# Offsets made between the steps of the value projection, half of the columns normalised on GpSimd, far sums turned later

## The chip, the cores and the metric

The kernel runs on one NeuronCore of one Trainium2 chip. A NeuronCore has TensorE (matmuls into PSUM), VectorE, ScalarE and GpSimd (elementwise work) and SyncE, which here only issues DMAs; each works through its own queue in order, and they wait for one another on semaphores. The metric is the time of one execution on the device in microseconds (us), as the median of several runs. Lower is better.

## The reference

The input x is float32, 2 images of 128 channels by 128 by 128 pixels. Two blocks follow each other, each with a residual:

```python
x = x + window_attention(group_norm(x))        # windows of 16 x 16, 8 heads, a bias table
x = x + deformable_conv(group_norm(x))         # the part that the change touches
```

The deformable convolution, with G = 8 groups of 16 channels and K = 9 points (3 x 3):

```python
v  = xt @ value_proj_w.T + value_proj_b                   # value projection
om = xt @ offset_mask_w.T + offset_mask_b                 # per pixel, group, point: dx, dy, mask
loc_x = px + kx + off[..., 0];  loc_y = py + ky + off[..., 1]
# bilinear sample of v at (loc_y, loc_x), four corners, zero outside the image
out = einsum('nhwkgc,nhwkg->nhwgc', sampled, mask)        # sum over the 9 points
out = out @ output_proj_w.T + output_proj_b
```

## The kernel before

The attention block runs first (functions above line 726) and takes about half of the time. `deformable` (line 726) then treats the two images one after the other (`Fori(0, B)` on every engine). For an image:

1. **Projection of the attention's output and the residual.** The sum stays in SBUF as `x1`; `cols` is a view of it by image columns. Group norm statistics are taken on the way; `gn` holds scale and shift of each channel.
2. **Value projection**, 32 steps v of four image columns (`COLS = 4`, `GROUPS = 32`). ScalarE normalises four columns into one half of `d_xn` (line 1357), TensorE multiplies them by the value weights (L1248) into one half of `sum_ps`, VectorE adds the bias into a row buffer in the memory of `vring` (L1460), and SyncE stores it to `vals` in DRAM (L976). There are two row buffers.
3. **A prefix** for the first six groups (`LEAD = 6`). Per group of four columns: TensorE makes offsets and masks (`offsets`, L1257 and L1260) in `om_ps`; ScalarE copies them to `off` (L1381) and takes absolute values (L1384); VectorE looks for far points, those over one pixel off (`find_far`, L1471 to L1476). For groups 0 and 1 ScalarE also makes the hat functions (`hats`, L1390 and L1394), and for group 0 VectorE makes the tap terms (`tap_terms`, L1515 and L1520) and TensorE the tap weights (`weights`, L1270 and L1275). Meanwhile SyncE loads the first seven columns of `vals` into the ring of eight, `vring` (L985), and stores the offsets (L995).
4. **The sampling loop** over 32 groups, written out for eight and looped over in the middle (`each_group`). For each of the four columns r of a group, VectorE multiplies 5 x 5 shifted values by the weights (`products`, L1536, in pieces, into two alternating halves of `prod`), and TensorE adds them up and transposes them into `sum_ps` (`taps`, 25 matmuls, L1297). Between the columns of a group stand, in this order: on TensorE the turn of the far sums of the group before (`turn`, L1307) after column 0, the weights of the next group after 1, the output projection of the group before (`project`, L1315) and the offsets of group q + 7 after 2, with the count of far points (L1285) once per epoch; on VectorE the result of group q - 2 (`result`, L1547) after 0, the tap terms of the next group after 1, the search for far points of group q + 6 after 2, in one group of four also the flags (L1487 to L1496), and after column 3 `read_counts` (L1502), which waits for that count.
5. **Far points.** Once per epoch of four groups GpSimd reads the number of rounds and does them (`far_round`, L1113 to L1163): it fetches one far point per partition and round from DRAM, gathers its corners from `vals`, and scatters the weighted sum into `far_sums`. `far_done` tells that an epoch is finished. SyncE loads a group's far sums into `fsum` (`load_far`, L1006), and waits for `far_done` before it (L1002). All columns that it loads later stand behind this wait in its queue. The groups 0 to 3 are epoch 0; the count of epoch 1 is read in group 1, that of epoch 7 in group 25.
6. **The end**: the last results, then the stores of `x1` to `out`.

GpSimd has nothing to do in steps 2 and 3. The order on each engine is written out by hand.

## Time and profile before

| | |
|---|---|
| Median of 3 runs | 3354.45 us (3354.16 to 3354.75) |
| Profiled execution: time, span | 3350.4 us, 3348.7 us |
| TensorE (PE) busy | 2717.4 us, 81% |
| VectorE (DVE) busy | 2716.9 us, 81% |
| ScalarE (ACT) busy | 1882.3 us, 56% |
| GpSimd (POOL) busy | 1102.7 us, 33% |
| Mean granted TensorE clock | 0.963 of full speed |
| Value projection, image 0 and image 1 begin | 1647.9 us, about 2549.5 us |
| First product of the sampling loop, image 0 and 1 | 1737.5 us, 2640.9 us |
| VectorE waits for "DMA vring<-vals" in the loop | 49.2 us in total |

Busy time says only that an engine executes; what a change is worth is read from the stage, from what ends last there. In the timelines the last part in brackets is the idle time of the engine before the row, and the instruction or transfer that ended it. Several instructions of one line that follow closely are merged, and "x4" tells how many they are.

### The profile page before, as it was taken

The numbers are of one execution on the slowest core, as the hardware profiler recorded it, in microseconds if no ns is written. First come the engines' busy times: TensorE is split into PE (matmuls) and PEld (weight loads), VectorE is DVE, ScalarE is ACT, GpSimd is POOL, SyncE is SP. The second block draws the span as 40 slices with busy tenths as digits, with TensorE's granted clock in tenths as the row PEclk, the third lists the DMA queues.
The fourth block names the chain that finished last, engine by engine and source line by source line (L and its number), as shares of the span: only waits on it lengthen the run. The fifth ranks groups of instructions, "written<-read, shape, count | busy, mean of one in ns | idle before, by whom it ended". The sixth has DMA issues, their size and how long they took to land.

```text
span 3348.7 us, 78453 instructions
## 1 busy us (share of the span) xinstructions
PE 2717.4 (81%) x22424; PEld 2178.8 (65%) x22424; DVE 2716.9 (81%) x6553; ACT 1882.3 (56%) x3529; POOL 1102.7 (33%) x1525
## 2 busy tenths in 40 slices
PE   0599999999999999995665999897856699989886
PEld 0355655565556655563555888887845598888885
DVE  5488888888888888885656999998945599999996
ACT  0488888888888888885262444442204544434420
POOL 0333333333333333332415322135421241115550
PEclk9999999999999999998898999998978899999998
DMA  6788888888888888885642333233365333333334
GB/s 221 126 142 140 146 136 142 139 144 137 143 139 147 136 142 138 141 143 109 199 138 84 99 97 98 93 99 88 89 242 160 110 118 94 96 96 98 105 91 161
DMA packets 350617, 432.47 MB, mean 129 GB/s; under 512 B 42224, under 2 KB 275072, under 8 KB 344304
## 3 DMA queue, kind: packets, MB, share of 16 engines
q1 hardware_dynamic: 338544, 423.85, 56.5%
q0 software_dynamic: 11904, 6.44, 1.6%
q8 instruction: 97, 1.59, 0.2%
q14 instruction: 72, 0.59, 0.1%
HBM read 283.33 MB, written 147.09 MB: 129 GB/s over the span
## 4 chain that ended last, share of the span: by engine, by line
DVE 19%; DMA 8%; issue 8%; PE 6%; POOL 6%; POOLq 2%; DVEq 1%; ACT 1%; SPq 1%; ACTq 0%
DVE prod L1536 11%; DVE tt L1520 2%; PE sum_ps L1297 2%; DMA vring<-vals 2%; DMA vals<-vring 2%; DMA vring<-attended 2%; DVE x L1547 2%; POOL gath L1113 2%; POOLq L1120 1%; PE wt_ps L1275 1%; DMA o_sel<-off_out,pos 1%; DVE my L1515 1%; PE sum_ps L1237 1%; POOL i_sel L1113 1%; PE om_ps L1260 1%
## 5 line engine op out<-in xcount | busy, mean ns | idle before, releaser
L587 ACT ACTIVATE prob<-sbias,nmax 128x256 f32<-128x256 f32 x2048 | 905.0, 501 | 196.1 <-DVE nmax L674 194.1
L1536 DVE TENSOR_TENSOR prod<-vring,wt_ps 128x1920 f32<-128x1920 f32 (+3 forms) x512 | 902.7, 1816 | 58.9 <-DMA vring<-vals 49.2
L674 DVE CUSTOM_DVE_ANT_0 sbias<-s_ps,nbias 128x256 f32<-128x256 f32 x2048 | 766.9, 421 | 224.3 <-PE s_ps L479 211.8
L1297 PE MATMUL sum_ps<-d_ident,prod 128*128 128x128 f32 x6400 | 758.7, 276 | 23.5 <-DVE prod L1536 23.5
L492 PE MATMUL pt_ps<-a_ident,prob 128*128 128x128 f32 x4096 | 644.3, 280 | 134.1 <-ACT prob L587 131.6
L1297 PEld LDWEIGHTS sum_ps<-d_ident,prod 128*128 128x128 f32 x6400 | 721.4, 143 | 38.4 <-DVE prod L1536 31.6
L492 PEld LDWEIGHTS pt_ps<-a_ident,prob 128*128 128x128 f32 x4096 | 447.3, 140 | 277.6 <-DVE probT L683 118.4
L479 PE MATMUL s_ps<-stack 96*128 96x256 bf16 x2048 | 396.2, 274 | 9.5 <-DMA stack<-parts_dram 9.5
L683 DVE COPY probT<-pt_ps 128x512 f32<-128x512 f32 x512 | 351.7, 687 | 11.8 <-PE pt_ps L492 11.7
L423 POOL CAST parts<-qk 128x1024 bf16<-128x1024 f32 x64 | 66.3, 1036 | 860.1 <-ACT qk L580 860.1
L1403 ACT COPY ssum<-sum_ps 128x512 f32<-128x512 f32 x64 | 37.5, 586 | 513.6 <-PE sum_ps L1307 513.6
L1275 PE MATMUL wt_ps<-tt,d_ident 128*128 128x144 f32 x2304 | 312.0, 291 | 0.0
L1275 PEld LDWEIGHTS wt_ps<-tt,d_ident 128*128 128x128 f32 x2304 | 306.9, 195 | 0.9
L479 PEld LDWEIGHTS s_ps<-stack 96*128 96x128 bf16 x2048 | 174.8, 98 | 203.5 <-issue 137.0
L594 ACT COPY probT<-pt_ps 128x512 f32<-128x512 f32 x512 | 290.2, 567 | 0.0
L507 PE MATMUL o_ps<-probT,va 128*32 128x256 f32 x4096 | 274.1, 385 | 0.9 <-DVE probT L683 0.9
L1128 POOL COPY first_e<-first_at 128x2 f32 x16 | 2.8, 178 | 784.3 <-issue 784.3
L1390 ACT ACTIVATE hat<-off,one_col 128x576 f32<-128x576 f32 x128 | 140.5, 1098 | 198.2 <-DVE tt L1520 198.2
L1520 DVE TENSOR_TENSOR tt<-hat,my 128x864 f32<-128x864 f32 x192 | 192.4, 1057 | 9.1 <-PE wt_ps L1275 0.5
L674 DVE DVE_READ_ACCUMULATOR2_ANT nmax<- 128x1 f32 x2048 | 170.8, 83 | 0.0
L1381 ACT COPY off<-om_ps 128x864 f32<-128x864 f32 x64 | 56.3, 880 | 202.6 <-PE om_ps L1260 184.9
L507 PEld LDWEIGHTS o_ps<-probT,va 128*32 128x32 f32 x4096 | 106.9, 109 | 87.8 <-issue 33.9
(166 smaller groups left out, 3489.9 us busy)
## 6 DMA issues: line engine op xcount, KB each, us to landing
stack<-parts_dram SPq DMA_DIRECT2D x768, 128.0 KB, 7.4
vring<-vals SPq DMA_DIRECT2D x270, 320.0 KB
parts_dram<-parts SPq DMA_DIRECT2D x64, 768.0 KB, 6.5
off_out<-off SPq DMA_DIRECT2D x64, 432.0 KB
strips<-x SPq DMA_DIRECT2D x68, 256.0 KB, 3.6
a_stats_in<-x SPq DMA_DIRECT2D x16, 1024.0 KB, 4.9
far_sums<-nothing SPq DMA_DIRECT2D x64, 256.0 KB, 2.1
attended<-on SPq DMA_DIRECT2D x256, 64.0 KB
```

The source lines that it names most:

```text
L479: mm = nc.tensor.matmul(s_ps[:, n % 2, half, :], stack[:, par, 0, h, at:at + P], stack[:, par, 1, h, w * NT:(w + 1) * NT], start=True, sto ...
L492: mm = nc.tensor.transpose(pt_ps[:, T_BANK[n % 4], kh, half * P:(half + 1) * P], prob[:, n % 4, half, kh * P:(kh + 1) * P], ident[:])
L507: mm = nc.tensor.matmul(o_ps[32 * j:32 * j + VA, t * NT:(t + 1) * NT], va[:, par, 2 * w + kh, 4 * t + j, :], probT[:, (4 * k + j) % 8, kh, ...
L587: ins = nc.scalar.activation(prob[:, n % 4, half, :], sbias[:, n % SBIAS, half, :], ACT.Exp, bias=nmax[:, n % SBIAS, half:half + 1], scale ...
L594: nc.scalar.copy(probT[:, n % 8], pt_ps[:, T_BANK[n % 4]]).then_inc(t_read_a, 1)
L674: ins = nc.vector.tensor_tensor_reduce(out=sbias[:, n % SBIAS, half, :], in0=s_ps[:, n % 2, half, :], in1=nbias[:, h, half, :], scale=1.0, ...
L683: nc.vector.tensor_copy(probT[:, n % 8], pt_ps[:, T_BANK[n % 4]]).then_inc(t_read_v, 1)
L1275: mm = nc.tensor.matmul(acc[:, :, jx:jx + KS, jy * G:(jy + KS) * G], ident[:], tt[:, jx, jy, 2 * half:2 * half + 2].rearrange("p r (a k) - ...
L1297: mm = nc.tensor.matmul(sum_ps[:, par, r * H:(r + 1) * H], prod[:, r % 2, dx, dy * C:(dy + 1) * C], ident[:], start=(r + dx + dy == 0), st ...
L1390: nc.scalar.activation(xy(hat[:, j]), xy_off(s), ACT.Abs, bias=0.0 if j == 1 else one_col[:, j // 2:j // 2 + 1]).then_inc(dist_ready, 1)
L1520: ins = nc.vector.tensor_tensor(tt[:, jx], hat[:, jx, :, 0:KG].unsqueeze(1) .to_broadcast([P, 3, COLS, KG]), my[:], ALU.mult)
L1536: nc.vector.tensor_tensor(prod[:, r % 2, first:last].rearrange("p a (t c) -> p (a t) c", c=CG), vring[:, at:at + wide].rearrange("p a (t c ...
```

## The change

- The value projection has four row buffers (`VROWS = 4`) in place of two. Its 32 steps are no longer a loop over pairs but go through `each_step`: eight written out, sixteen in a loop of four, eight written out (`V_FIRST, V_LAST = 8, 24`).
- Odd steps are normalised by GpSimd, even ones by ScalarE, each with a semaphore of its own.
- TensorE makes the offsets of groups 0 to 6 after the value matmuls of steps 1 to 7, from the half of `d_xn` that the step before has used; they are not normalised again. ScalarE reads offsets 0 to 5 in steps 2 to 7; VectorE looks for far points of groups 0 to 4 in steps 3 to 7 and of group 5 in step 24; hats, tap terms, counts and the weights of group 0 are cut up over steps 24 to 31. The prefix is gone.
- SyncE stores offsets in steps 4 to 7 and 24, 25, and loads the first four columns in step 24. GpSimd waits for all stores of values before its far rounds, as SyncE does before the other columns.
- In the loop, the load of the far sums of group q goes from column 2 of group q to column 1 of group q + 1; `turn` of the group before goes from after column 0 to after column 2; `project` is of group q - 2 in place of q - 1, after column 0; `result` goes from after column 0 to after column 2. ScalarE's order in a group is offsets, hats, sums, normalisation; it was offsets, normalisation, sums, hats.

```diff
+VROWS = 4
+V_FIRST, V_LAST = 8, 24
+AHEAD_OFF = LEAD + 1
...
+vrow = vring[:, ATTS:ATTS + VROWS, 0:COLS * C].rearrange("p s (r c) -> p s r c", c=C)
 off = sb("off", [P, RING_O, COLS, KG, 3])
...
+def each_step(eng, body):
+for v in range(V_FIRST):
+    body(v, v % VROWS, v // VROWS)
+with eng.Fori(0, (V_LAST - V_FIRST) // VROWS) as i:
+    for u in range(VROWS):
+        body(VROWS * i + V_FIRST + u, u, i + V_FIRST // VROWS)
+for v in range(V_LAST, GROUPS):
+    body(v, v % VROWS, v // VROWS)
...
-    for n in range(AHEAD_V):
+    def store_values(v, slot, turn):
+        sp.wait_ge(vrow_ready, count(b * GROUPS + v + 2))
+        sp.dma_start(at(vals, ((PAD + v * COLS) * YP + PAD) * C,
+                        [[C, P], [YP * C, COLS], [1, C]]), vrow[:, slot]).then_inc(vrow_out[slot], 16)
+        if isinstance(v, int) and 0 <= v - EPOCH < V_FIRST - EPOCH:
+            store_offsets(first_spot(v - EPOCH))
+        if isinstance(v, int) and 0 <= v - V_LAST < LEAD - (V_FIRST - EPOCH):
+            store_offsets(first_spot(v - V_LAST + V_FIRST - EPOCH))
+        if isinstance(v, int) and v == V_LAST:
+            for n in range(2):
+                sp.wait_ge(vrow_out[n], count(b * (4 * GROUPS) + 16))
+                sp.sem_inc(sp_passed, 1)
+            for n in range(ATTS):
+                load_column(n, n, b * LOADS[n % 2] + n // 2)
+    each_step(sp, store_values)
+    for slot in range(VROWS):
+        sp.wait_ge(vrow_out[slot], count((b + 1) * (4 * GROUPS)))
+        sp.sem_inc(sp_passed, 1)
+    for n in range(ATTS, AHEAD_V):
...
-    for q in range(LEAD):
-        store_offsets(first_spot(q))
...
-            if r == 2:
-                load_far(s)
+            if r == 1 and s.has(-1):
+                load_far(s.on(-1))
     each_group(sp, columns)
+    load_far(first_spot(GROUPS - 1))
     sp.wait_ge(res_ready, count((b + 1) * GROUPS))
...
                 nc.gpsimd.tensor_tensor(rows, rows, bproj_sb[:].unsqueeze(1).to_broadcast([P, COLS, W]),
                                         ALU.add).then_inc(b_added, 1)
+    pool.wait_ge(g_sq, count(2 * b + 2))
+    pool.sem_inc(pool_passed, 1)
+    def normalise(v):
+        pool.wait_ge(v_done, count(b * GROUPS + v))
+        pool.sem_inc(pool_passed, 1)
+        if 2 <= v < AHEAD_OFF + 2:
+            pool.wait_ge(om_done, count(b * GROUPS + v - 1))
+            pool.sem_inc(pool_passed, 1)
+        nc.gpsimd.tensor_scalar(xn[:, 1], cols[:, v * COLS:(v + 1) * COLS, :], gn[:, 0:1], gn[:, 1:2],
+                                ALU.mult, ALU.add).then_inc(vn_ready[1], 1)
+    for v in range(1, GROUPS, 2):
+        normalise(v)
+    for slot in range(VROWS):
+        pool.wait_ge(vrow_out[slot], count((b + 1) * (4 * GROUPS)))
+        pool.sem_inc(pool_passed, 1)
...
     def offsets(q, par):
         n = b * GROUPS + q
-        pe.wait_ge(xn_ready, count(n + 1))
+        if not isinstance(q, int) or q >= AHEAD_OFF:
+            pe.wait_ge(xn_ready, count(b * (GROUPS - AHEAD_OFF) + q - AHEAD_OFF + 1))
         pe.wait_ge(off_ready, count(n))
         for half in range(HALVES):
...
-        if s.has(-LAG):
-            turn(s.on(-LAG))
+        if s.has(-2 * LAG):
+            project(s.on(-2 * LAG))
         taps(s.q, par, 1)
         if s.has(1):
             weights(s.on(1).q, 0)
         taps(s.q, par, 2)
         if s.has(-LAG):
-            project(s.on(-LAG))
+            turn(s.on(-LAG))
         if s.has(LEAD + 1):
             offsets(s.on(LEAD + 1).q, (s.place + LEAD + 1) % 2)
         if s.has(LEAD) and (s.place + LEAD) % EPOCH == EPOCH - 1:
             count_far(s.on(LEAD).epoch)
         taps(s.q, par, 3)
-    for q in range(LEAD + 1):
-        offsets(q, q % 2)
-    count_far(0)
-    weights(0, 0)
+    def value(v, slot, turn):
+        par = slot % 2
+        pe.wait_ge(vn_ready[par], count(b * (GROUPS // 2) + turn * (VROWS // 2) + slot // 2 + 1))
+        pe.wait_ge(vrow_ready, count(b * GROUPS + v))
+        for r in range(COLS):
+            mm = nc.tensor.matmul(sum_ps[:, par, r * C:(r + 1) * C], xn[:, par, r, :], wvalue_sb[:],
+                                  start=True, stop=True)
+        mm.then_inc(v_done, 1)
+        if isinstance(v, int):
+            if 0 <= v - 1 < AHEAD_OFF:
+                offsets(v - 1, (v - 1) % 2)
+            if v == V_LAST:
+                count_far(0)
+            if v == GROUPS - 2:
+                weights(0, 0)
+    each_step(pe, value)
     each_group(pe, group)
     turn(first_spot(GROUPS - 1))
-    project(first_spot(GROUPS - 1))
+    for q in range(GROUPS - 2 * LAG, GROUPS):
...
     def group(s):
         if s.has(LEAD):
             read_offsets(s.on(LEAD))
+        if s.has(2):
+            hats(s.on(2))
+        if s.has(-LAG):
+            read_sums(s.on(-LAG).q, (s.place - LAG) % RING_S)
         if s.has(LEAD + 2):
             normalise(s.on(LEAD + 2).q, (s.place + LEAD + 2) % 2, b * GROUPS + s.q + LEAD + 1)
-        if s.has(-LAG):
-            read_sums(s.on(-LAG).q, (s.place - LAG) % RING_S)
-        if s.has(2):
-            hats(s.on(2))
-    normalise(0, 0, b * GROUPS)
-    normalise(1, 1, b * GROUPS)
-    for q in range(2, LEAD + 2):
-        read_offsets(first_spot(q - 2))
-        normalise(q, q % 2, b * GROUPS + q - 1)
-        if q == 2:
-            hats(first_spot(0))
-    hats(first_spot(1))
+    def value(v, slot, turn):
+        if slot % 2 == 0:
+            act.wait_ge(v_done, count(b * GROUPS + v))
+            if not isinstance(v, int):
+                act.wait_ge(om_done, count(b * GROUPS + AHEAD_OFF))
+            elif 2 <= v < AHEAD_OFF + 2:
+                act.wait_ge(om_done, count(b * GROUPS + v - 1))
+            src = cols[:, v * COLS:(v + 1) * COLS, :] if isinstance(v, int) else \
+                cols[:, bass.ds(v * COLS, COLS), :]
+            nc.scalar.activation(xn[:, 0], src, ACT.Identity, bias=gn[:, 1:2],
+                                 scale=gn[:, 0:1]).then_inc(vn_ready[0], 1)
+        if isinstance(v, int):
+            if 0 <= v - 2 < LEAD:
+                read_offsets(first_spot(v - 2))
+            if V_LAST <= v < V_LAST + 3:
+                hats(first_spot(0), range(2 * (v - V_LAST), 2 * (v - V_LAST) + 2))
+            if GROUPS - 3 <= v:
+                hats(first_spot(1), range(2 * (v - GROUPS + 3), 2 * (v - GROUPS + 3) + 2))
+    each_step(act, value)
+    act.wait_ge(v_done, count((b + 1) * GROUPS + 1))
+    normalise(LEAD + 1, (LEAD + 1) % 2, b * GROUPS + LEAD)
     each_group(act, group)
     read_sums(GROUPS - 1, (GROUPS - 1) % RING_S)
...
-        if s.has(-RES_LAG):
-            result(s.on(-RES_LAG).q)
         products(s.q, par, 1)
         if s.has(1):
             tap_terms(s.on(1))
         products(s.q, par, 2)
+        if s.has(-RES_LAG):
+            result(s.on(-RES_LAG).q)
         if s.has(LEAD):
...
-    for q in range(LEAD):
-        find_far(first_spot(q))
-        if q == 0:
-            tap_terms(first_spot(0))
-        if q == EPOCH - 1:
-            flags(first_spot(q))
-    read_counts(first_spot(0))
+    def value(v, slot, turn):
+        if isinstance(v, int) and 0 <= v - 3 < V_FIRST - 3:
+            find_far(first_spot(v - 3))
+        if isinstance(v, int) and 0 <= v - V_LAST < LEAD - (V_FIRST - 3):
+            find_far(first_spot(v - V_LAST + V_FIRST - 3))
+        dve.wait_ge(v_done, count(b * GROUPS + v + 2))
+        dve.wait_ge(vrow_out[slot], count(b * (4 * GROUPS) + 16 * turn))
+        nc.vector.tensor_tensor(vrow[:, slot], sum_ps[:, slot % 2].rearrange("p (r c) -> p r c", c=C),
+                                bvalue_sb[:].unsqueeze(1).to_broadcast([P, COLS, C]),
+                                ALU.add).then_inc(vrow_ready, 1)
+        if isinstance(v, int):
+            if v - 3 == EPOCH - 1:
+                flags(first_spot(v - 3))
+            if v == V_LAST + 1:
+                read_counts(first_spot(0))
+            if v == V_LAST + 3:
+                tap_terms(first_spot(0))
+    each_step(dve, value)
     each_group(dve, group)
     for q in range(GROUPS - RES_LAG, GROUPS):
         result(q)
```

## Rows read from the trace of the kernel before

**Rows 1.** Two stretches: us, each engine's busy us (instructions), TensorE clock, DMA share, GB/s
```profile
1675.00:1704.70 29.70, 17.40 (x134) 15.75 (x133) 11.88 (x18) 20.25 (x17) 0.00 (x0) 0.98 0.53 159
...
1811.70:1897.40 85.70, 76.56 (x622) 72.30 (x621) 84.38 (x75) 34.75 (x40) 40.09 (x72) 1.00 0.34 101
```

**Rows 2.** VectorE timeline, both value projections: start, us, engine, line, operands, [idle before]
```profile
1651.60 0.69 DVE L1460 TENSOR_TENSOR vring<-sum_ps,bvalue_sb 128x512 f32<-128x512 f32 x1 [4.03 <-PE sum_ps L1248]
...
1690.27 0.69 DVE L1460 TENSOR_TENSOR vring<-sum_ps,bvalue_sb 128x512 f32<-128x512 f32 x1 [1.83 <-DMA vals<-vring]
...
1693.68 0.69 DVE L1460 TENSOR_TENSOR vring<-sum_ps,bvalue_sb 128x512 f32<-128x512 f32 x1 [1.82 <-DMA vals<-vring]
...
2553.22 0.69 DVE L1460 TENSOR_TENSOR vring<-sum_ps,bvalue_sb 128x512 f32<-128x512 f32 x1 [4.04 <-PE sum_ps L1248]
```

**Rows 3.** VectorE timeline, the first groups of each image and a later stop
```profile
1737.48 7.01 DVE L1536 TENSOR_TENSOR prod<-vring,wt_ps 128x1920 f32<-128x1920 f32 x4 [2.11 <-PE wt_ps L1275]
...
1745.60 3.00 DVE L1520 TENSOR_TENSOR tt<-hat,my 128x864 f32<-128x864 f32 x3
...
1794.40 3.55 DVE L1536 TENSOR_TENSOR prod<-vring,wt_ps 128x1280 f32<-128x1280 f32 x2 [26.47 <-DMA vring<-vals]
...
1807.39 0.15 DVE L1502 TENSOR_SCALAR some<-few_ps 1x8 f32<-1x8 f32 x1 [2.29 <-PE few_ps L1285]
...
2326.00 3.55 DVE L1536 TENSOR_TENSOR prod<-vring,wt_ps 128x1280 f32<-128x1280 f32 x2 [13.73 <-DMA vring<-vals]
...
2640.90 7.02 DVE L1536 TENSOR_TENSOR prod<-vring,wt_ps 128x1920 f32<-128x1920 f32 x4 [2.15 <-PE wt_ps L1275]
...
2680.06 3.55 DVE L1536 TENSOR_TENSOR prod<-vring,wt_ps 128x1280 f32<-128x1280 f32 x2 [8.74 <-DMA vring<-vals]
```

**Rows 4.** SyncE queue timeline, loads of the far sums
```profile
1790.51 0.39 SPq L1006 DMA_DIRECT2D fsum<-far_sums  x1
...
2321.65 0.39 SPq L1006 DMA_DIRECT2D fsum<-far_sums  x1
...
2676.22 0.39 SPq L1006 DMA_DIRECT2D fsum<-far_sums  x1
```

**Rows 5.** GpSimd timeline, far rounds of the first epoch
```profile
1736.94 0.18 POOL L1128 COPY first_e<-first_at 128x2 f32 x1 [102.89 <-issue]
...
1745.67 2.01 POOL L1142 TENSOR_SCALAR idxf<-low,i_sel 128x1 f32<-128x1 f32 x1
...
1761.97 0.27 POOL L1142 TENSOR_SCALAR idxf<-low,i_sel 128x1 f32<-128x1 f32 x1
...
2640.07 0.18 POOL L1128 COPY first_e<-first_at 128x2 f32 x1 [104.48 <-issue]
```

**Rows 6.** GpSimd groups by line
```profile
L414 POOL TENSOR_SCALAR xn<-xraw,a_gnp 128x512 f32<-128x512 f32 x64 | 49.2, 769 | 19.8 <-POOL a_gnp L407 19.8
```

**Rows 7.** ScalarE timeline, value projection and offsets
```profile
1647.92 2.41 ACT L1357 ACTIVATE d_xn<-x,d_gn 128x512 f32 x2 [2.10 <-DVE d_gn L157]
...
1710.53 1.05 ACT L1390 ACTIVATE hat<-off,one_col 128x576 f32<-128x576 f32 x1
...
1715.28 0.86 ACT L1381 COPY off<-om_ps 128x864 f32<-128x864 f32 x1
```

**Rows 8.** TensorE timeline
```profile
1701.36 1.13 PE L1248 MATMUL sum_ps<-wvalue_sb,d_xn 128*128 128x128 f32 x8 [1.40 <-DVE vring L1460]
...
1704.33 1.64 PE L1260 MATMUL om_ps<-wom_sb,d_xn 128*128 128x216 f32 x4
...
1708.76 0.89 PE L1260 MATMUL om_ps<-wom_sb,d_xn 128*128 128x216 f32 x4
...
1801.67 2.89 PE L1297 MATMUL sum_ps<-d_ident,prod 128*128 128x128 f32 x25
...
1820.95 2.37 PE L1275 MATMUL wt_ps<-tt,d_ident 128*128 128x144 f32 x18
```

**Rows 9.** VectorE timeline, last row of the first image
```profile
2453.65 1.33 DVE L1547 SCALAR_TENSOR_TENSOR x<-out_ps,bout_sb,x 128x512 f32<-128x512 f32 x1 [3.43 <-PE out_ps L1315]
```

More of the change, by code:

```diff
@@ L843, in deformable @@
         g_sq = sem("g_sq")
-        vn_ready = sem("vn_ready")
+        vn_ready = [sem("vn_ready0"), sem("vn_ready1")]
         v_done = sem("dv_done")
         vrow_ready = sem("vrow_ready")
-        vrow_out = [sem("vrow_out0"), sem("vrow_out1")]
+        vrow_out = [sem(f"vrow_out{n}") for n in range(VROWS)]
         v_in = [sem("v_in0"), sem("v_in1")]
```

45 lines of the change are left out of this document (7 added, 38 removed).

## The prediction

> **What bounds the kernel now.** Read first the page's slices: VectorE is nine tenths busy in the last stage, except where it dips, from 1674 us to 1842, around 2300, and again from 2430 to 2680. The table of stretches says the same: in four groups of the sampling loop VectorE is busy for 84.4 of 85.7 us and TensorE for 76.6, while in the value projection VectorE has 11.9 of 29.7 [rows 1]. The loop is VectorE's; the change leaves all its instructions there in place, so time can come only from the stretches in which VectorE waits. The timeline of VectorE then gives those, and the queue of SyncE and the timeline of GpSimd say why:
> (a) The value projection goes at the pace of its stores. An add that reuses a buffer follows the last one by 3.41 us (1690.27 to 1693.68), waits on the store, and two steps pass in that time: 1.7 us a step, 32 steps [rows 2].
> (b) Then come the offsets of the first six groups, with nothing beside them. Counting from the first normalisation (1647.92 [rows 7], which is 3.68 before the first add), the first product starts at 89.6 in image 0; in image 1, whose first add is at 2553.22, at 2640.90, which is 91.4 [rows 2, 3].
> (c) In group 1, VectorE stops for 26.47 us for columns that SyncE cannot issue, because the load of far sums stands ahead of them in its queue until GpSimd has done the far rounds of epoch 0; the sums are loaded at 1790.51, 53.6 us after the rounds began at 1736.94. Behind it comes a wait of 2.29 us for the counts of epoch 1. Image 1 stops for 8.74, with rounds of 36.2 us (2640.07 to 2676.22). The same happens in image 0 in front of 2326.00: 13.73 us [rows 3 to 5].
>
> **The change part by part.** Time t runs from the first normalisation of an image, n is a value step, E the end of the last add, T0 the first product.
> *Steps 0 to 8.* Here each step also issues the offsets of the group before, and the next normalisation waits for them, since both read the same half of d_xn. So TensorE and the normaliser take turns. Prices: normalisation on ScalarE 1.2 plus 0.15 to be seen (two in 2.41 [rows 7]); on GpSimd the trace has the same operation and shape at 0.77 [rows 6]; four value matmuls 0.56, half of 1.13 [rows 8]; one group's offsets are two halves of 0.89 and their bias matmuls, 2.1, or 3.5 where the half takes 1.64 at the lower clock [rows 8]; the copy out of PSUM 0.86 to 0.9 [rows 7], which in even steps comes behind ScalarE's normalisation and ahead of the next offsets. The first step is as before (add at 3.68), value 1 ends at about 5.1, offsets 0 at the low clock at 8.6, offsets 1 after 1.4 + 1.1 + 3.5 at 14.6. Then five more, at the high clock: 0.77 + 0.3 + 0.56 + 2.1 = 3.7 for a GpSimd step, 1.4 + 0.9 + 2.1 = 4.4 for a ScalarE step; 3.7 three times and 4.4 twice are 19.9. Offsets 6 end at 34.5. If the clock stays low all through (the trace has both), the five cost 28 to 29.
> *Steps 8 to 23.* Four store buffers instead of two take the store off the path: 3.41 per four steps. What then ends last is ScalarE's lane, one even step: 1.4 + 0.56 + 0.2 = 2.15 for two, 1.07 a step, 17.1 for sixteen. The stores would then move 256 KB in 1.07 us; they now take a DMA share of 0.53 at 159 GB/s [rows 1], so this needs about 0.8. Bounds: 1.07, and the old 1.7, which is 10 us more. Step 24's normalisation starts at 51.6.
> *Steps 24 to 31.* The hats of groups 0 and 1 are cut up between them; six instructions take 4.75 (1710.53 to 1715.28 [rows 7]). Two pieces of hats 0 and two normalisations bring add 27 to about 8.3 after the start of step 24; the tap terms behind it are four operations of 1.0 (three in 3.00 [rows 3]), 4.2 with their gaps, to 12.5; hats 1 wait for them, 1.6; normalisation 30 waits behind these, to 15.4; value 30, the weights of group 0 (2.4 [rows 8], or double at the low clock after this pause) and value 31, add: 20 to 23. I take 22. E = 73.6. The four column loads that SyncE now issues at step 24 hold up its stores for some 4 us, within what four buffers cover.
> *To T0.* Last store 2.7 (3.41 less the add's 0.69), then column 4 must land, 3.2 to 3.9 (1790.51 to 1794.40, two issues): T0 = E + 6.1 = 79.7. That is 9.9 us earlier in image 0 and 11.7 in image 1.
> *Normalising on GpSimd.* It removes 16 of ScalarE's 32, in the sum above. The trace shows what GpSimd can lose beside VectorE: one operation on 128x1 takes 2.01 us exactly while VectorE multiplies hat by my, both in SBUF, and 0.27 otherwise [rows 3, 5]. In the odd steps 3, 5 and 7 and in step 25 VectorE has a search for far points (1.4 us) that can meet the normalisation: 0 to 5.6 us per image; I take 0, as GpSimd has slack to ScalarE's lane in all but the first steps.
> The Trainium skill (GPSIMD Engine Reference, section 1, Specifications) says that GpSimd shares its SBUF interfaces with VectorE and contends with VectorE's instructions that have two SBUF inputs. By that rule this part costs up to the upper end just given, and the sum below would be 3318; the 2.01 us agree with the rule, but whether the two meet in these steps no trace here shows.
> *Far sums later.* The load moves from column 2 of its own group to column 1 of the next, three columns on, and the transposes from after tap 0 to after tap 2. GpSimd may start its rounds when the last store has landed and the count is read: E + 3.9. If they last 53.6 as before, image 0's sums are loaded at E + 57.5 = T0 + 51.4. Columns then no longer end last (VectorE would lack one at about T0 + 44.6 only), but TensorE's queue does: its transposes stand ahead of offsets 8 and of the count for epoch 1, which VectorE wants at T0 + 41.2 (30.45 to the old stop, 10.7 from 1794.40 to 1807.39 less 2.29 [rows 3]). 3.2 for the load, 1.1 for the transposes, 3.5 for offsets at low clock, 0.3: the count is read at T0 + 59.5. Before it was T0 + 69.9 (1807.39). Gain 10.4; a stop of some 18 us stays, under another name. Image 1: rounds of 36.2 load the sums at T0 + 34.0, before the transposes are due; the 8.7 go. The stop before 2326.00: its sums were loaded at 2321.65; the flags now come behind a result, 1.3 later, so the count would be read at 2321.65 + 1.3 + 3.2 + 1.1 + 0.6 = 2327.9, while without a stop VectorE would be there at 2312.27 + 10.7 + 1.3 = 2324.3. 3.6 stay, 10.1 go.
> *Order in the loop.* Nothing is added. A product step needs 3.5 (7.01 for two), 25 taps 2.89, and TensorE has 9 us to spare in four groups [rows 1, 3, 8]. With the result moved, VectorE now does products 3, 0 and 1 in a row, and products 1 must find taps 3 done: they have 3.5 us for 2.9, less with the piece that starts early. Cost 0, bounds 0 and 1 us a group.
> *End of each image.* Result 30 has to leave PSUM before the last projection; the last result waits 3.43 us now [rows 9] and will wait for a projection, a result and a projection more: +1.8 each, 3.6.
> Sum: 9.9 + 10.4 + 10.1 + 11.7 + 8.7 - 3.6 = 47.2. Profiled execution 3350.4, so 3303.2; the median of the runs is 4.05 above it: **3307**.
>
> **The rivals.**
> A. *The clock and the stores hold the projection back.* Low clock through steps 2 to 8 (+9), a slow tail (+1) and the old 1.7 per step (+10) in both images: 40 less, 3347. For it: every second stretch of offsets in the trace is slow. Against it: with stores at 1.7 the granted clock was 0.98, the higher level nearly throughout [rows 1].
> B. *Everything quick.* High clock from the first offsets (-4) and a tail of 18 (-4), both images, and no remainder at 2326 (-4): 3287.
> C. *The loop's order costs (slower).* If taps 3 with offsets and transposes in front of them make products 1 wait, 62 groups pay. From 0.76 us a group it eats the 47; at 1.2 us it is 74, and the time 3307 + 74 = 3381. For it: at the low clock 25 taps take nearly double, as the offsets' half does (1.64 for 0.89 [rows 8]), and the 3.5 us don't hold them. Against: the granted clock is 1.00 in the loop and TensorE idle for a tenth [rows 1].
> D. *The projection gains nothing but the loads later do*: the first steps in turns plus the slow tail use up all that the stores give: 21.6 less, 3329.
>
> **How the numbers follow.** Forecast 0.50, B 0.17, D 0.15, A 0.11, C 0.07. A measurement tells 0.2%, 6.7 us, from no change. Half of A lies inside that: faster 0.88, same 0.05, slower 0.07. The range leaves out C, most of A and the far end of B: 3283 to 3332.
>
> **What would show it.** VectorE's first product about 80 us after the first normalisation in both images; adds about 1.1 us apart from step 9 and about 4 before; the columns no longer named as what VectorE waits for in group 1, but the count on few_ps, some 18 us in image 0 and none in image 1; groups at 20.6 us as before. It is wrong if the first product is not earlier, if the far rounds take much over 53.6 us, or if VectorE waits in each group for TensorE's taps.

## The result, and the profile after

| | before | after |
|---|---|---|
| Median (range, runs) | 3354.4 us (3354.16 to 3358.95, 6) | 3333.55 us (3319.04 to 3337.56, 6) |
| Ratio after / before | | 0.9928, 95% interval 0.9913 to 0.9943 |
| Profiled execution: time, span | 3350.4, 3348.7 us | 3319.04, 3317.4 us |

The change makes the kernel 0.7% faster, 24 us by the ratio. 3307 was forecast, so half of the gain of 47 us came. By the ratio the time is 3330.3 on the scale of the first median, at the upper end of the range (3283 to 3332); the bare median of after lies 1.6 above it. The profiled execution is the quickest of its six, so the trace below accounts for 31 us rather than 24.

Stretches of the new value projection and of the same four groups of the sampling loop as in [rows 1], with the same columns:

```profile
1650.00:1681.50 31.50, 22.29 (x129) 19.21 (x127) 14.78 (x30) 14.65 (x15) 4.88 (x4) 0.95 0.30 102
1681.50:1704.70 23.20, 16.47 (x129) 14.96 (x128) 10.40 (x16) 11.14 (x9) 8.51 (x7) 1.00 0.61 187
...
1811.70:1897.40 85.70, 78.45 (x613) 73.83 (x612) 84.07 (x75) 33.43 (x39) 39.40 (x71) 0.96 0.33 101
```

In the loop VectorE is as busy as before (84.1 of 85.7 us): a group still takes 20.6 us, and 24.1 with the flags, as before. In the projection the granted clock is 0.95 and 1.00 of full speed in the two stretches, so nearly all of it is at the higher level; the low clock of rival A is not there.

VectorE's timeline in the projection, which answers to [rows 2], up to the first product:

```profile
1657.04 0.69 DVE L1621 TENSOR_TENSOR vring<-sum_ps,bvalue_sb 128x512 f32<-128x512 f32 x1 [4.17 <-PE sum_ps L1375]
...
1661.57 0.69 DVE L1621 TENSOR_TENSOR vring<-sum_ps,bvalue_sb 128x512 f32<-128x512 f32 x1 [2.44 <-PE sum_ps L1375]
...
1666.06 0.69 DVE L1621 TENSOR_TENSOR vring<-sum_ps,bvalue_sb 128x512 f32<-128x512 f32 x1 [2.47 <-PE sum_ps L1375]
...
1684.48 1.40 DVE L1621 TENSOR_TENSOR vring<-sum_ps,bvalue_sb 128x512 f32<-128x512 f32 x2 [4.00 <-PE sum_ps L1375]
...
1690.05 1.41 DVE L1621 TENSOR_TENSOR vring<-sum_ps,bvalue_sb 128x512 f32<-128x512 f32 x2 [1.41 <-PE sum_ps L1375]
...
1727.33 0.69 DVE L1621 TENSOR_TENSOR vring<-sum_ps,bvalue_sb 128x512 f32<-128x512 f32 x1 [3.29 <-PE sum_ps L1375]
1733.59 7.01 DVE L1581 TENSOR_TENSOR prod<-vring,wt_ps 128x1920 f32<-128x1920 f32 x4 [5.57 <-DMA vring<-vals]
```

Early adds are 4.5 us apart (1657.04, 1661.57, 1666.06), where 3.7 and 4.4 in turn were forecast. From step 8 on four of them take 5.57 us (1684.48 to 1690.05), 1.39 a step, where 1.07 was forecast; the add waits for matmuls, no longer for a store. The tail after step 24 holds stops of 3 to 4 us, and the first product waits 5.57 for column 4.

VectorE's timeline behind it: the counts read in group 1, later in image 0 and in group 1 of image 1, the end of image 0, and image 1's first product, which answer to [rows 3, 9]:

```profile
1790.51 0.15 DVE L1547 TENSOR_SCALAR some<-few_ps 1x8 f32<-1x8 f32 x1 [15.84 <-PE few_ps L1318]
...
2312.26 0.15 DVE L1547 TENSOR_SCALAR some<-few_ps 1x8 f32<-1x8 f32 x1 [1.73 <-PE few_ps L1318]
...
2428.92 1.33 DVE L1592 SCALAR_TENSOR_TENSOR x<-out_ps,bout_sb,x 128x512 f32<-128x512 f32 x1 [3.79 <-PE out_ps L1348]
...
2613.84 7.01 DVE L1581 TENSOR_TENSOR prod<-vring,wt_ps 128x1920 f32<-128x1920 f32 x4 [5.46 <-DMA vring<-vals]
...
2656.41 0.15 DVE L1547 TENSOR_SCALAR some<-few_ps 1x8 f32<-1x8 f32 x1 [1.50 <-PE few_ps L1318]
```

The wait for columns in group 1 (26.47) has become one of 15.84 for the count on `few_ps`, as forecast (18); the one of 13.73 has become 1.73; the one of 8.74 in image 1 is a wait of 1.50. At the end of image 0 the last two results now wait 3.79 and 1.28. SyncE's queue shows why, with the loads of [rows 4]:

```profile
1783.37 0.39 SPq L1011 DMA_DIRECT2D fsum<-far_sums  x1
...
2308.07 0.39 SPq L1011 DMA_DIRECT2D fsum<-far_sums  x1
```

The load of the sums is issued 49.8 us after the first product (1733.59); 51.4 was forecast. Columns are ahead of that load in the queue now, so only TensorE's transposes, and the count behind them in its queue, wait for it.

For accounts by stage I use five marks: *gn* (VectorE has made the coefficients of the second group norm, 0.1 to 0.4 us before the first normalisation), *E* (last value add ends), *T0* (first product), *c1* (the count of the next epoch is read, in group 1), *end* (last result of the image). In us, from VectorE's timeline, image 0 / image 1:

| kernel | gn | E - gn | T0 - gn | c1 - T0 | end - c1 |
|---|---|---|---|---|---|
| before | 1647.6 / 2549.2 | 57.1 / 57.0 | 89.9 / 91.7 | 69.9 / 51.4 | 647.6 / 633.5 |
| after | 1646.9 / 2526.9 | 81.1 / 81.5 | 86.7 / 87.0 | 56.9 / 42.6 | 642.4 / 638.6 |
| after, again | 1652.2 / 2532.7 | 82.1 / 82.2 | 87.5 / 87.6 | 57.3 / 45.6 | 643.2 / 639.5 |
| value_only | 1650.7 / 2548.4 | 81.3 / 81.3 | 86.8 / 86.8 | 65.5 / 51.6 | 652.3 / 636.8 |
| loop_only | 1650.9 / 2542.0 | 57.0 / 56.8 | 90.1 / 89.9 | 60.9 / 41.0 | 643.1 / 636.1 |
| no_pool | 1651.1 / 2540.1 | 85.0 / 83.2 | 90.5 / 88.9 | 60.7 / 41.0 | 646.4 / 639.9 |
| xn4 | 1648.9 / 2523.2 | 70.5 / 70.1 | 76.2 / 75.8 | 57.5 / 46.6 | 646.0 / 639.2 |
| tail20 | 1650.3 / 2527.7 | 78.6 / 80.2 | 84.2 / 85.6 | 57.4 / 46.3 | 642.3 / 636.7 |
| turn_last | 1649.4 / 2524.1 | 82.6 / 82.0 | 88.1 / 87.8 | 41.0 / 41.0 | 649.9 / 641.8 |
| rows4 | 1651.3 / 2548.6 | 46.9 / 46.1 | 79.9 / 80.2 | 69.8 / 52.4 | 649.0 / 634.2 |
| rows4_loop | 1649.8 / 2520.2 | 46.0 / 46.0 | 80.1 / 80.1 | 41.0 / 41.0 | 650.7 / 640.3 |
| best | 1651.9 / 2515.3 | 68.4 / 68.1 | 74.1 / 73.3 | 41.0 / 41.0 | 652.3 / 639.8 |
| pad | 1646.5 / 2533.9 | 81.3 / 81.4 | 87.5 / 87.1 | 57.8 / 42.7 | 643.8 / 637.3 |

41.0 is the floor of c1 - T0: no stop at all.

### The profile page after: what moved, and what is told of

Same layout as the page of the kernel before. It is cut to its first block, busy times and chain, and to the rows that moved or that the text cites. A ratio compares the mean times of both kernels' runs of the same rounds, so it can differ in the third digit from the quotient of the medians.

```text
span 3317.4 us, 78066 instructions
## 1 busy us (share of the span) xinstructions
PE 2731.6 (82%) x22424; PEld 2191.1 (66%) x22424; DVE 2720.6 (82%) x6553; ACT 1827.6 (55%) x3483; POOL 1151.6 (35%) x1557
## 3 DMA queue, kind: packets, MB, share of 16 engines
q1 hardware_dynamic: 338544, 423.85, 57.5%
## 4 chain that ended last, share of the span: by engine, by line
DVE 24%; issue 10%; DMA 7%; PE 5%; POOL 3%; DVEq 1%; ACT 1%; POOLq 1%; SPq 1%; ACTq 0%
DVE prod L1581 17%; DMA vring<-vals 3%; DVE tt L1565 2%; PE sum_ps L1375 2%; DVE my L1560 2%; DMA vring<-attended 1%; DVE x L1592 1%; PE sum_ps L1330 1%; ACT d_xn L1464 1%; PE sum_ps L1279 1%; PE om_ps L1293 1%; POOL gath L1155 1%; POOLq L1162 1%; DMA o_sel<-off_out,pos 1%; DMA out<-x 1%
## 5 line engine op out<-in xcount | busy, mean ns | idle before, releaser
L1330 PE MATMUL sum_ps<-d_ident,prod 128*128 128x128 f32 x6400 | 772.0, 278 | 81.7 <-DVE prod L1581 81.6
L1330 PEld LDWEIGHTS sum_ps<-d_ident,prod 128*128 128x128 f32 x6400 | 731.2, 144 | 130.1 <-DVE prod L1581 103.2
L1279 PE MATMUL sum_ps<-wproj_sb,vring 128*128 128x128 f32 x512 | 80.2, 317 | 88.5 <-DMA vring<-attended 79.3
L429 POOL TENSOR_TENSOR rest<-qk,parts 128x1024 f32<-128x1024 f32 x64 | 137.1, 2142 | 11.8 <-POOL parts L426 11.8
```

The lines of the kernel that those rows point to most:

```text
L1330: mm = nc.tensor.matmul(sum_ps[:, par, r * H:(r + 1) * H], prod[:, r % 2, dx, dy * C:(dy + 1) * C], ident[:], start=(r + dx + dy == 0), st ...
```

## The experiments

Each kernel has its ratio to the kernel before, which ran beside it; the number in brackets is the 95% interval.

**again**: the changed kernel, unaltered, run a second time.

> The changed kernel unaltered, to see what its scatter is made of: six runs lay at 3319 to 3338 us, while those of the kernel before lie within 1 us but for one. Theory F: the two jumps back in TensorE's instruction loop wait for instructions (3.3 and 2.0 us idle with no releaser in the profiled run, the quickest) and vary; then a profile of a slower run shows more or longer idle of that kind, some 14 us of it, in the loop. Theory G: the far rounds vary; then the stop before the counts in group 1 (15.8 us) and that near 2312 (1.7 us) are longer in a slower run, and the groups between are of equal length.

3332.28 us, ratio 0.9927 (0.9914 to 0.9940); the kernel before has 3355.55 (3351.08 to 3362.33, 17 runs). The gain is the same. Of the 10.5 us by which this profile is longer than that of after, 5.3 lie in the attention, which the change does not touch (gn 1652.2), and 3.0 in the rounds of image 1 (45.6 for 42.6). TensorE's stops in group 16 (pad, below) cost VectorE 2.31 and 3.34 here, 4.14 and 2.79 in after, and the stop at 2312 is 4.86 for 1.73. So half of the difference between these two profiles lies outside the change and the rest in far rounds. Theory F is wrong: its waits are shorter in the slower profile. What causes the scatter stays open; value_only (3345.45 to 3358.42), loop_only (3329.24 to 3340.57) and the kernel before scatter by 11 to 13 us too, so it needs no part of the change.

**value_only**: the new projection with the old order in the loop, edits in this pattern on every engine:

```diff
                     products(s.q, par, 0)
+                    if s.has(-RES_LAG):
+                        result(s.on(-RES_LAG).q)
                     products(s.q, par, 1)
...
-                        if r == 1 and s.has(-1):
-                            load_far(s.on(-1))
+                        if r == 2:
+                            load_far(s)
```

> The new value projection with the loop in the old order (far sums loaded at column 2 of their own group, turned after column 0, results after column 0). My account of the traces gives the projection 3.0 us in image 0 and 4.5 in image 1, and 0.9 each for far rounds that start earlier against the first product: 9 us, ratio 0.997, 3345 us, with the columns' stops of 26, 13 and 9 us back. Scatter: if the loop's order makes it, these runs lie within 2 us; if the projection does, they spread over 15 us.

**loop_only**: the reverse, the old projection and prefix with the new order in the loop.

> The old value projection and prefix with the loop in the new order. By the account 12 us of the first stop, 12 near 2312, 8.7 in image 1, less 3.1 at the ends and 6.9 for the two instruction waits of TensorE: 23 us, ratio 0.993, 3331 us. If the loop's order makes the scatter, these runs spread over 15 us and the median may be as low a gain as 10 us; if it doesn't they lie within 2 us. Rival: far rounds and value stage need each other, then it gives under 8 us.

value_only 3351.54 us, ratio 0.9990 (0.9980 to 0.9999); loop_only 3334.03, 0.9934 (0.9919 to 0.9948). The product is 0.9924, again is at 0.9927: the parts add up, and nearly all of the gain is the order in the loop. VectorE in group 1 of value_only, and of loop_only:

```profile
1790.83 3.55 DVE L1579 TENSOR_TENSOR prod<-vring,wt_ps 128x1280 f32<-128x1280 f32 x2 [22.90 <-DMA vring<-vals]
```

```profile
1801.88 0.15 DVE L1504 TENSOR_SCALAR some<-few_ps 1x8 f32<-1x8 f32 x1 [19.53 <-PE few_ps L1286]
```

The old stop is back in the first. In the second its name is the count and it is 19.5 long: the new order alone does nearly what the whole change does.

The marks show that the new projection does gain, and where that goes. In value_only the counts are read 7.5 us (image 0) and 4.7 us (image 1) sooner after gn than in the kernel before, and 8.0 of these 12.2 us are lost behind them. 7.0 of the 8.0 are one place, group 16 in both images, where VectorE waits for the tap weights, 3.94 and 3.09 us:

```profile
2115.97 3.00 DVE L1563 TENSOR_TENSOR tt<-hat,my 128x864 f32<-128x864 f32 x3 [3.94 <-PE wt_ps L1307]
```

The kernel before and loop_only have no such wait of VectorE's, rows4 has 0.70 and 0.50; after has it, 4.14 and 2.79 (pad, below). So of what the new projection wins ahead of the loop, TensorE's stop in group 16 takes back more than half in value_only; loop_only and again are 1.75 us apart, within their intervals.

**no_pool**: ScalarE normalises all 32 steps.

```diff
-                for v in range(1, GROUPS, 2):
-                    normalise(v)
...
-                    if slot % 2 == 0:
+                    if True:
```

> The changed kernel with all 32 steps normalised on ScalarE. Mine: GpSimd buys nothing. Steps 8 to 23 take 1.39 us with it, and ScalarE alone needs 1.2 us a step with two halves to work in; steps 2 to 8 stay at 4.5; ratio to the changed kernel 0.999 to 1.001. Rival: GpSimd's half is what lets steps pass in 1.39 us; without it 1.7 to 2.3 us a step for the 16 to 24 steps, 10 to 20 us slower in both images.

3337.02 us, ratio 0.9945 (0.9931 to 0.9960). Its adds in image 1:

```profile
2582.68 0.69 DVE L1619 TENSOR_TENSOR vring<-sum_ps,bvalue_sb 128x512 f32<-128x512 f32 x1 [1.08 <-PE sum_ps L1373]
...
2588.17 0.69 DVE L1619 TENSOR_TENSOR vring<-sum_ps,bvalue_sb 128x512 f32<-128x512 f32 x1 [1.07 <-PE sum_ps L1373]
```

Four steps take 5.49 us, with GpSimd 5.57: from step 8 to step 24 GpSimd brings nothing, and ahead of step 8 as good as nothing: the add of step 8 comes 37.9 and 37.1 us after gn here, 37.6 and 37.9 in after. The 2 to 4 us of T0 - gn that it does bring lie in the tail, where ScalarE also makes the hats: from the add of step 24 to E it takes 24.1 and 24.0 us here, 20.8 in after. The medians of no_pool and again stand at 1.0014, where 0.999 to 1.001 was expected; the intervals overlap. The rival's 10 to 20 us are not there.

**pool_rows**: GpSimd reads its 512 values from adjacent addresses (`x1`), where `cols` has them 128 apart.

```diff
-nc.gpsimd.tensor_scalar(xn[:, 1], cols[:, v * COLS:(v + 1) * COLS, :], gn[:, 0:1], gn[:, 1:2],
+nc.gpsimd.tensor_scalar(xn[:, 1], x1[:, v * (COLS * H):(v + 1) * (COLS * H)].rearrange(
+                            "p (r h) -> p r h", h=H), gn[:, 0:1], gn[:, 1:2],
```

> The changed kernel, but GpSimd reads 512 adjacent values of x1 in place of four image columns, whose values lie 128 apart; the value projection of half the columns is thus that of other pixels. Mine: the operation takes 1.21 us in the changed kernel and 0.77 in the attention block because of the distance between values, so here it takes 0.77 to 0.80; but from step 8 on the lane of ScalarE (1.28 + 0.18 + 1.05 + 0.27 = 2.78 for two steps) sets the pace, so only steps 3, 5 and 7 gain 0.45 each: the last add comes 79.8 us after the coefficients in place of 81.1 to 82.1, and the time is within 3 us of the changed kernel's. Rival: GpSimd's lane sets the pace, and 24 steps gain 0.2 each, 5 us an image. Other rival: the 1.21 are contention with VectorE and stay.

4935.67 us, ratio 1.4693: the values and offsets of the odd steps come from other pixels, so this is no longer the same computation; far more points are far, and GpSimd's rounds swamp the time, which says nothing here. The trace does. The line's view (ns min/median/max), and VectorE's adds 2 to 4 and two later ones:

```profile
L1127 POOL TENSOR_SCALAR d_xn<-x,d_gn x32: 762/768/2687, 1651.5 to 2648.9; 128x512 f32<-128x512 f32 x32
```

```profile
1660.60 0.69 DVE L1622 TENSOR_TENSOR vring<-sum_ps,bvalue_sb 128x512 f32<-128x512 f32 x1 [3.70 <-PE sum_ps L1376]
...
1664.69 0.69 DVE L1622 TENSOR_TENSOR vring<-sum_ps,bvalue_sb 128x512 f32<-128x512 f32 x1 [1.99 <-PE sum_ps L1376]
...
1669.17 0.69 DVE L1622 TENSOR_TENSOR vring<-sum_ps,bvalue_sb 128x512 f32<-128x512 f32 x1 [2.47 <-PE sum_ps L1376]
...
1686.73 1.40 DVE L1622 TENSOR_TENSOR vring<-sum_ps,bvalue_sb 128x512 f32<-128x512 f32 x2 [3.99 <-PE sum_ps L1376]
...
1692.28 1.41 DVE L1622 TENSOR_TENSOR vring<-sum_ps,bvalue_sb 128x512 f32<-128x512 f32 x2 [1.42 <-PE sum_ps L1376]
```

768 ns where after has 1217 at the median: the spacing costs 0.45 us. A step that GpSimd normalises takes 4.09 (1660.60 to 1664.69) for 4.53 in after, one of ScalarE 4.48, and the pairs from step 8 on still take 5.55 per four. So from step 8 on GpSimd's duration doesn't count, and before it it does, by 0.44 a step of its own. The last add comes 78.9 us after gn, where 79.8 was expected. The 1.21 us are not contention with VectorE, which was the other rival: VectorE's work is the same here.

**xn4**: four places for normalised columns in place of two (the other two in `prod`, idle at that time).

```diff
+        xv = [xn[:, 0], xn[:, 1], spare[:, 0], spare[:, 1]]
...
-                        act.wait_ge(v_done, count(b * GROUPS + v))
+                        act.wait_ge(v_done, count(b * GROUPS + v - (min(v, 2) if isinstance(v, int) else 2)))
...
-                        elif 2 <= v < AHEAD_OFF + 2:
-                            act.wait_ge(om_done, count(b * GROUPS + v - 1))
+                        elif 4 <= v < AHEAD_OFF + 4:
+                            act.wait_ge(om_done, count(b * GROUPS + v - 3))
```

> The changed kernel with four places for normalised columns in place of two (the two more lie in memory of prod, unused until the first product). Mine: steps 2 to 8 are 4.45 us because normalising, value matmuls and offsets follow one another; with four places the normalising is out of the row, and 1.05 + 1.83 + the wait for the copy give 3.0 to 3.2; steps 8 to 24 go from 1.39 to TensorE's 1.05 to 1.1. Last add 81 -> 66 to 68 us after the coefficients, first product with it, in both images: 26 to 30 us, ratio to the kernel before 0.984 to 0.985. Rival: the value stores or VectorE hold the pace (1.3 us a step) and the first part gains alone: 18 us.

3308.80 us, ratio 0.9852 (0.9835 to 0.9869). TensorE's timeline:

```profile
1679.46 3.42 PE L1378 MATMUL sum_ps<-wvalue_sb,d_xn 128*128 128x128 f32 x16 [3.32 <-ACT d_xn L1467]
...
1684.81 2.05 PE L1378 MATMUL sum_ps<-wvalue_sb,d_xn 128*128 128x128 f32 x16
1686.93 2.05 PE L1378 MATMUL sum_ps<-wvalue_sb,prod 128*128 128x128 f32 x16
1688.88 2.05 PE L1378 MATMUL sum_ps<-wvalue_sb,d_xn 128*128 128x128 f32 x16
```

Sixteen matmul records in 2.05 us, and nothing between the rows: TensorE itself is the bound, at 1.02 a step. The two halves of `sum_ps`, the adds and the stores are as in after, so none of them held the pace of 1.39. T0 - gn falls by 10.5 and 11.2. E - gn of 70.5 is above the 66 to 68 that I expected, for the wait of 3.32 ahead of step 8, where ScalarE's `size` waits behind VectorE's flags.

**tail20**: the tail starts at step 20, so hats 1 can start at step 26 (`V_FIRST, V_LAST = 8, 20`).

> The changed kernel with the last written-out part begun at step 20 in place of 24, so that hats and tap terms of group 0 come four steps earlier and hats of group 1 at steps 26 to 28. Mine: the eight steps from 24 take 24.3 us, most of it ScalarE's wait for tap terms and the weights behind value 30 at the low clock; over twelve steps the same work hides better, and the last add comes 5 to 8 us earlier: 76 to 73 after 81 to 82, both images, 10 to 16 us in all. Rival: the work simply adds up on ScalarE (hats 9.5, normalising 1.28 each), and it gains under 3 us.

3321.59 us, ratio 0.9893 (0.9876 to 0.9910). E - gn falls by 1.3 to 2.5, where 5 to 8 was expected. Besides, VectorE's waits at the loop's end are gone (see pad).

**turn_last**: the far sums are turned behind taps 3, behind the count.

```diff
-                    if s.has(-LAG):
-                        turn(s.on(-LAG))
                     if s.has(LEAD) and s.on(LEAD).place == 3:
...
                     taps(s.q, par, 3)
+                    if s.has(-LAG):
+                        turn(s.on(-LAG))
```

> The changed kernel with the turn of far sums one place later on TensorE, behind the count and behind taps of column 3. Mine: the stop of 15.8 us in front of the counts in group 1 is TensorE's queue waiting for far sums with offsets and count behind it. Then the counts are read at 42 us after the first product in place of 57, and a smaller stop of 8 to 10 us comes in group 2, where tap terms and products wait for weights behind the turn; the later stop of 2 to 5 and that in image 1 go. 10 to 14 us less than the changed kernel, ratio to before 0.989. Rival: the far rounds bind either way and the stop only moves: under 4 us.

3318.03 us, ratio 0.9880 (0.9863 to 0.9896). c1 - T0 is 41.0 in both images. Group 2 now has a stop:

```profile
1791.14 3.55 DVE L1581 TENSOR_TENSOR prod<-vring,wt_ps 128x1920 f32<-128x1920 f32 x2 [8.29 <-DMA vring<-vals]
```

Columns again: the load of far sums stands ahead of them in SyncE's queue. Of the 15.84, 8.29 are left, in their third place. The ratio to the changed kernel is 0.9952, 16 us; 10 to 14 was expected.

**rows4**: the kernel before with four row buffers and nothing else of the change.

```diff
-                with sp.Fori(0, GROUPS // 2) as i:
-                    for par in range(2):
+                with sp.Fori(0, GROUPS // 4) as i:
+                    for par in range(4):
```

> The kernel before with four row buffers in place of two, and nothing else of the change: offsets stay in the prefix, ScalarE normalises all columns. Mine: the gain of the changed projection is the store's alone, and making offsets between the steps gives it back. Without GpSimd the steps passed in 1.37 us (profile of no_pool), so 32 steps at 1.37 for 1.71 make the first product come 79 to 80 us after the coefficients in place of 90 (87 in the changed kernel): 20 us in both images, ratio 0.994. Rival: four stores under way land later and the step stays near 1.6: 6 us.

3338.75 us, ratio 0.9945 (0.9931 to 0.9958). Its adds:

```profile
1674.93 0.69 DVE L1460 TENSOR_TENSOR vring<-sum_ps,bvalue_sb 128x512 f32<-128x512 f32 x1 [0.91 <-PE sum_ps L1248]
1676.02 0.69 DVE L1460 TENSOR_TENSOR vring<-sum_ps,bvalue_sb 128x512 f32<-128x512 f32 x1 [0.40 <-PE sum_ps L1248]
1677.80 0.69 DVE L1460 TENSOR_TENSOR vring<-sum_ps,bvalue_sb 128x512 f32<-128x512 f32 x1 [1.08 <-PE sum_ps L1248]
1678.72 0.69 DVE L1460 TENSOR_TENSOR vring<-sum_ps,bvalue_sb 128x512 f32<-128x512 f32 x1 [0.23 <-PE sum_ps L1248]
1680.32 0.69 DVE L1460 TENSOR_TENSOR vring<-sum_ps,bvalue_sb 128x512 f32<-128x512 f32 x1 [0.91 <-PE sum_ps L1248]
```

Four steps in 5.39 us with ScalarE alone, and T0 - gn is 79.9, seven less than in after. The store buffers alone give 10 to 11.5 us an image; putting the offsets between the value steps gives 7 of them back.

**rows4_loop**: rows4 with the new order in the loop and turn_last.

> rows4 with the loop in the new order and the turn of far sums last on TensorE. If the parts add up: 0.994 x 0.9934 (loop alone) x 0.9953 (turn_last against the changed kernel) = 0.983, 3298 us, faster than the changed kernel by 30 us with the plain prefix kept. Rival: with the first product earlier the far rounds bind more, and 10 us less comes of it: 0.986.

3308.78 us, ratio 0.9859 (0.9843 to 0.9876), as the rival in that text had it (0.986), not 0.983. The stop for columns in group 2 is 12.37 us, for 8.29 in turn_last, whose first product is 8 us later.

**best**: xn4, tail20 and turn_last together.

> The changed kernel with xn4, tail20 and turn_last together. First product 73 us after the coefficients (76 in xn4, 3 less for the tail), counts read 41 us behind it, a stop of 8 to 9 us in image 0. 0.9852 less 0.0034 for the tail and 0.0047 for the turn: 0.977, 3280 us. Rival: turn and tail gained on the same waits and only one counts: 0.981.

3287.85 us, ratio 0.9793 (0.9780 to 0.9805): the quickest here, 2.1% below the kernel before and 1.4% below the changed one; it lies between the 0.977 expected and the rival's 0.981. Its largest stop:

```profile
1783.09 3.55 DVE L1584 TENSOR_TENSOR prod<-vring,wt_ps 128x1920 f32<-128x1920 f32 x2 [11.73 <-DMA vring<-vals]
```

Still the column loads behind the far sums, 11.73 us.

**pad**: the changed kernel with 40 `pe.sem_inc` on TensorE ahead of the loop over groups; nobody waits for them.

> The changed kernel with 40 more semaphore increments (2.5 KB of instructions at a guess of 64 bytes each) in TensorE's queue ahead of the loop. Mine: the waits of TensorE with no releaser where its loop jumps back (3.3 and 2.0 us in the middle of the weights, 4.1 and 2.8 for VectorE) depend on where the loop's instructions lie, since they were absent in loop_only and tail20, which have the same loop elsewhere; moved by 40 they fall at another instruction: VectorE's stop at that place changes by over 1 us or goes, in both images. Rival: they come from the order within the group, and stay at 2 to 4.5 us at the same weights.

3324.15 us, ratio 0.9900 (0.9883 to 0.9916). First TensorE and VectorE of after where the written-out groups begin again, then of pad:

```profile
2095.28 0.34 PE L1303 MATMUL wt_ps<-no_col,bom_ones 128*128 128x400 bf16 x1 [2.02 <-issue]
2095.45 0.78 PE L1308 MATMUL wt_ps<-tt,d_ident 128*128 128x144 f32 x5
2099.51 3.28 PE L1308 MATMUL wt_ps<-tt,d_ident 128*128 128x144 f32 x13 [3.29 <-issue]
...
2102.83 2.99 DVE L1565 TENSOR_TENSOR tt<-hat,my 128x864 f32<-128x864 f32 x3 [4.14 <-PE wt_ps L1308]
```

```profile
2097.15 0.51 PE L1304 MATMUL wt_ps<-no_col,bom_ones 128*128 128x400 bf16 x1 [2.94 <-issue]
2097.45 3.69 PE L1309 MATMUL wt_ps<-tt,d_ident 128*128 128x144 f32 x18
...
2101.18 3.00 DVE L1568 TENSOR_TENSOR tt<-hat,my 128x864 f32<-128x864 f32 x3 [1.54 <-PE wt_ps L1309]
```

In after TensorE stops twice with no releaser that the profile names, the second time in the midst of the tap weights, and VectorE waits 4.14 us (2.79 at the same place in image 1). In pad the stop is ahead of the weights, and VectorE's wait is 1.54, and none in image 1. In tail20 the stop is ahead of them too (2.45 and 2.32), and loop_only has one in image 1 (2.04): what is absent in those two is VectorE's wait, not TensorE's stop, as the expectation above has it. Forty instructions that do nothing move it, so it hangs on where the instructions lie. (They take TensorE 4.0 us ahead of the loop, while VectorE waits for columns anyway.) In the kernel before, TensorE has one such stop as well (2.85 ahead of the weights at 2112.35, 2.87 in image 1), and VectorE none.

The trace has a row that bears on it: the DMA queue of kind "instruction". In after, in 40 us of the loop (2040 to 2080) and in the 14 us around the stop (2088 to 2102), its packets, MB and share of the DMA engines are:

```profile
q8 instruction: 2, 0.03, 0.4%
...
q8 instruction: 4, 0.07, 2.6%
```

Twice the packets in a third of the time, just where the loop jumps back: this agrees with TensorE waiting for its own instructions. The row doesn't name the engine that they are for, so it supports this reading and doesn't prove it.

The intervals of pad and after touch, so a gain is not shown by them alone. Pad's profile is 6.1 us longer than that of after, the quickest of its six; against again it is 4.4 shorter (spans 3323.5 and 3327.9), with 4.1 less of these waits of VectorE's.

## Why the prediction was half right

- *Far sums later*: right, in the mechanism and in each size. c1 - T0 fell by 13.0 in image 0 (10.4 forecast) and 8.8 in image 1 (8.7); the stop at 2326 gave 12.0 (10.1). The 2.6 and 1.9 more: 1.6 us less from T0 to the load of the sums and 1.0 less from there to the count (7.1 for 8.1), and a remainder of 1.73 for 3.6. In again that remainder is 4.86, so the forecast lies within the scatter.
- *Steps 0 to 8*: the sum right, by errors that cancel. Offsets 6 end 34.5 us after the first normalisation, as forecast: GpSimd's normalisation takes 1.21 us, not 0.77, and a step's value matmuls 1.15, not 0.56, but the clock was at its higher level from offsets 1 on. I took the price from a row of the same shape and operation [rows 6] and did not look at the spacing of what it reads, which pool_rows settled. The Trainium skill (GPSIMD Engine Reference, section 7, Performance pitfalls for Q7 kernels) says of kernels written for GpSimd's cores that a read with a step over 8 bytes costs about half as much again per element. For the built-in operation here the ratio measured is 1217 / 768 = 1.58.
- *Steps 8 to 23*: the failed step. "Four value matmuls 0.56, half of 1.13" is wrong. A float32 product of `value` leaves two records in the profile, so "x8" in [rows 8] is one step, not two. The same line has 512 records in the 64 steps of the kernel before, eight a step for four products; that division would have shown it. A transpose leaves one: the 25 of `taps` are the "x25" of [rows 8]. ScalarE's lane is 1.28 + 0.18 + 1.05 + 0.27 = 2.78 for two steps, which one sees in ScalarE's, TensorE's and GpSimd's rows:

```profile
1687.21 1.27 ACT L1464 ACTIVATE d_xn<-x,d_gn 128x512 f32 x1 [1.53 <-PE sum_ps L1375]
...
1685.86 2.06 PE L1375 MATMUL sum_ps<-wvalue_sb,d_xn 128*128 128x128 f32 x16 [0.70 <-ACT d_xn L1464]
1688.68 2.05 PE L1375 MATMUL sum_ps<-wvalue_sb,d_xn 128*128 128x128 f32 x16 [0.77 <-DVE vring L1621]
...
1685.37 1.22 POOL L1127 TENSOR_SCALAR d_xn<-x,d_gn 128x512 f32<-128x512 f32 x1 [4.20 <-PE sum_ps L1375]
...
1715.60 3.35 POOL L1127 TENSOR_SCALAR d_xn<-x,d_gn 128x512 f32<-128x512 f32 x1 [1.63 <-PE sum_ps L1375]
```

ScalarE waits for step v's matmuls before it normalises v + 2, and TensorE for that normalisation: with two places each half goes round that circle, and who normalises hardly matters (no_pool). The forecast had this circle, with the matmuls in it at half of their price: with 1.05 in place of 0.56 its sum gives 2.65 for two steps. Cost against the forecast: 0.32 x 16 = 5.1 an image. xn4 opens the circle and goes at 1.02.
- *Steps 24 to 31*: 24.3 for 22, 2.3 more. To T0: 5.6 for 6.1. So the projection gave 3.2 and 4.7, not 9.9 and 11.7: rival D's mechanism (the projection gains nothing), with 3329 the nearest number, though for another reason than its slow tail.
- *Normalising on GpSimd*: one of its 16 operations takes 3.35 us, the others 1.22 (the row at 1715.60 above). At that time VectorE runs the tap terms, both inputs in SBUF:

```profile
1715.01 2.99 DVE L1565 TENSOR_TENSOR tt<-hat,my 128x864 f32<-128x864 f32 x3
```

The rule on the shared interfaces in the Trainium skill (GPSIMD Engine Reference, section 1, Specifications) agrees. GpSimd's own loss struck in step 31, where TensorE waits for ScalarE's hats longer, and cost nothing, as I had taken. But VectorE loses too, for which the forecast had no term:

```profile
1705.27 1.13 DVE L1516 TENSOR_TENSOR reach<-size 128x288 f32<-128x288 f32 x1
...
1713.18 1.70 DVE L1560 TENSOR_TENSOR my<-hat,mf 128x864 f32<-128x864 f32 x1
```

Both began while GpSimd normalised (1704.83 to 1706.08, 1712.74 to 1713.97); elsewhere they take 0.45 and 1.05, and in no_pool all do. With `far_at` at 1677.38 (1.06 for 0.17) that is 2.2 us of VectorE an image; what it costs in time no run separates.
- *Order in the loop*: cost 0, right; rival C is false, groups at 20.6 us.
- *End of each image*: 1.6 each for 1.8.
- *What I had no term for*: the stops of TensorE in group 16, 4.1 and 2.8 us of VectorE in the profile of after. They go with the new projection and the place that it gives the loop's instructions (3.9 and 3.1 in value_only, none in loop_only), so they take back most of the 7.9 us that the projection gives.

Together, against 47.2: projection 13.7 less, stops in group 16 6.9 less, far sums 4.6 more, the unchanged attention 0.7 more, rest within 1.5: 31 in the profile. The rest is scatter between executions: the profiled one of after is 14.5 below its median, that of before 4.0, which leaves 20.9 between the medians, and 24 by the ratio. That the total is still within the range owes something to luck: two errors in steps 0 to 8 cancelled, and the far sums gave 4.6 more than forecast.

## What to carry to other kernels

Count the records of a line against the steps that the code has before pricing one step by them. When a buffer pair is shared by a producer and a consumer that wait for each other, and nothing slower stands behind them, the pace is the round trip through both, and a second producer doesn't change it: count the places. Try the smallest part of a change by itself: four row buffers alone (rows4) brought the first product forward by 10.0 and 11.5 us, the whole new projection by 3.2 and 4.7. A load that waits for another engine should stand in its queue behind everything that doesn't need it; each time it, or the work on what it loads, was moved here, the stop came back smaller under another name.
